# All eight down matrices of the second expert loop loaded once, and picked by a register on TensorE

## The reference, cut to what matters

```python
router_logits = x @ gate_weight.T                      # 1024 tokens, 8 experts
probs = softmax(router_logits)
top_v, top_i = top_k(probs, 2)                          # weights normalised to sum 1
def expert_step(acc, (gu, dp, w)):
    gate, up = split(x @ gu.T, 2)                       # gu: 1024 x 256 of one expert
    hidden = silu(gate) * up                            # 512 wide
    return acc + w[:, None] * (hidden @ dp.T)           # dp: 256 x 512 of one expert
```

## Time and profile before

| what | value |
|---|---|
| median of 3 runs | 451.12 us (450.35 to 452.25) |
| time of the profiled execution | 449.55 us |
| its span, first to last instruction | 447.8 us |
| PE busy | 401.5 us (90%) |
| DVE busy | 328.8 us (73%) |
| POOL busy | 253.9 us (57%) |
| ACT busy | 236.9 us (53%) |
| HBM read, written | 71.76 MB, 5.24 MB |
| down matrices: issues, size, median to landing | 23, 512 KB, 5.3 us |
| gate and up matrices: the same | 22, 1024 KB, 7.8 us |

### The profile page before, as it was taken

How to read it: one execution, slowest core, us unless ns; L and a number is a source line. 1 busy time by engine, 2 the same in 40 slices (tenths; PEclk the granted TensorE clock), 3 DMA queues, 4 the chain that set the end, 5 groups by cost and what they waited for, 6 DMA issues and landing times.

```text
span 447.8 us, 6054 instructions
## 1 busy us (share of the span) xinstructions
PE 401.5 (90%) x1749; PEld 263.9 (59%) x1749; DVE 328.8 (73%) x620; ACT 236.9 (53%) x478; POOL 253.9 (57%) x352
## 2 busy tenths in 40 slices
PE   7798999999899999958885899999999999976895
PEld 6576788555555555626772456666665666653554
DVE  5998779999999999889877268548546411048994
ACT  5624683566676767569973222332333222349883
POOL 5474028577888997236614466976985463124641
PEclk9999999999999999998985899999999999999998
DMA  6900006365546565000024898999999985150011
GB/s 215 415 32 0 1 1 220 114 218 189 164 172 229 190 202 195 0 2 2 1 94 151 272 350 284 325 364 357 322 337 359 322 301 193 42 181 1 23 37 36
DMA packets 23664, 77.39 MB, mean 173 GB/s; under 512 B 3440, under 2 KB 7920, under 8 KB 20176
## 3 DMA queue, kind: packets, MB, share of 16 engines
q1 hardware_dynamic: 20336, 69.94, 44.1%
q0 software_dynamic: 2208, 6.03, 4.1%
q10 hardware_dynamic: 1088, 1.05, 0.7%
HBM read 71.76 MB, written 5.24 MB: 172 GB/s over the span
## 4 chain that ended last, share of the span: by engine, by line
PE 50%; DVE 27%; issue 12%; POOL 4%; ACT 3%; DMA 3%; SPq 0%; DVEq 0%; POOLq 0%; ACTq 0%
PE bank L1990 9%; PE bank L2021 9%; PE bank L2001 9%; DVE hx L1295 5%; PE bank L1770 5%; DVE fw L1084 4%; DVE bw L1087 3%; PE bank L1615 2%; PE bank L1617 2%; PE bank L1616 2%; PE bank L2012 2%; DVE fw L1092 2%; PE bank L1692 2%; DVE gl L1574 2%; PE bank L1839 1%
## 5 line engine op out<-in xcount | busy, mean ns | idle before, releaser
L1770 PE MATMUL bank<-hx,w2raw 128*128 128x512 f32 x128 | 67.2, 607 | 4.2 <-DVE hx L1295 3.3
L1510 DVE TENSOR_TENSOR hm<-bank,sl 128x512 f32<-128x512 f32 x23 | 15.8, 689 | 66.1 <-PE bank L2001 36.3
L808 ACT ACTIVATE rl<-bank 128x512 f32<-128x512 f32 x64 | 38.1, 595 | 37.9 <-PE bank L1617 37.1
L1615 PE MATMUL bank<-xlhi,w1hi 128*128 128x512 f32 x64 | 49.3, 771 | 0.0
L1990 PE MATMUL bank<-gu,xbT 128*128 128x512 f32 x92 | 45.4, 617 | 2.1 <-issue 1.6
L1295 DVE TENSOR_TENSOR hx<-bank,cwb 128x512 f32<-128x512 f32 x64 | 42.0, 658 | 3.1 <-ACT bank L812 2.9
L2021 PE MATMUL bank<-dn,hT 128*128 128x256 f32 x184 | 43.5, 379 | 0.4 <-ACT hT L931 0.4
L2021 PEld LDWEIGHTS bank<-dn,hT 128*128 128x128 f32 x184 | 34.9, 190 | 14.7 <-issue 11.1
L2001 PE MATMUL bank<-gu,xbT 128*128 128x512 f32 x92 | 43.3, 593 | 0.0
L589 POOL DMA_INDIRECT y_rows<-yb,dest_i x23 | 24.5, 1066 | 32.9 <-ACT yb L937 28.8
L937 ACT ACTIVATE yb<-bank 128x256 f32<-128x256 f32 x23 | 8.8, 384 | 60.8 <-PE bank L2021 60.8
(11 more groups left out here) (307 smaller groups left out, 961.3 us busy)
## 6 DMA issues: line engine op xcount, KB each, us to landing
gu<-in_gu SPq DMA_DIRECT2D x22, 1024.0 KB, 7.8
cwb<-cw_rows SPq DMA_DIRECT2D x32, 512.0 KB, 4.0
dn<-in_dn SPq DMA_DIRECT2D x23, 512.0 KB, 5.3
traw<-in_t SPq DMA_DIRECT2D x3, 1024.0 KB, 7.1
w1raw<-in_w SPq DMA_DIRECT2D x8, 256.0 KB, 4.7
w2raw<-in_w SPq DMA_DIRECT2D x8, 256.0 KB, 4.4
kT<-in_kt SPq DMA_DIRECT2D x4, 256.0 KB, 5.1
x<-in_x SPq DMA_DIRECT2D x2, 512.0 KB, 6.8
```

Of the source, the lines that this page charges most:

```text
L808: act.activation(rl[:, u % 3, :], bank[u % 4][:], ACT.Relu).then_inc(sem("r_ready"), 1)
L1615: pe.matmul(out, lhs[0], rhs[0], start=start, stop=False)
L1770: pe.matmul(bank[4 + s][:], w2raw[:, e // 4 % 2, e % 4, :], hx[:, 0, u % 4, :], start=(e == 0), stop=(e == E0 - 1), skip_group_check=True) ...
```

## The change

The tile `dn` now holds all eight down matrices (4 MB, 32 KB in each partition) and lies at the start of the region. `gu` comes behind it, and the tiles of layer 1 and 3 that lay behind both now begin at `gu`. SP loads the eight matrices with four DMAs of 1 MB right after the router's weights, when layer 0 is done (`x1_ready` 4). `down_weights` and its 23 loads, 23 register reads and 23 waits leave SP's list. TensorE reads the owner of block b - 1 into a register of its own in each pass with b of 1 or more, behind the transposes and ahead of `up(b)`, and `block_down` addresses the matrix with it. TensorE waits for the loads of `dn` once, at block 0.

```diff
@@ -172,8 +172,9 @@
 
 
         cursor[0] = region
+        dn = sb("dn", [P, E2, I2 // P, C])
+        first_region = cursor[0]
         gu = sb("gu", [P, RING, KC, 2 * I2])
-        dn = sb("dn", [P, RING, I2 // P, C])
         region2 = cursor[0]
 
 
@@ -195,7 +196,7 @@
         ends.append(cursor[0])
 
 
-        cursor[0] = region2
+        cursor[0] = first_region
         qf = sb("qf", [P, 2, C])
         qT = sb("qT", [P, 2, KC, P], BF16)
         xp = sb("xp", [P, 2, HID])
@@ -362,6 +363,9 @@
             ternary_in(0)
             sp.wait_ge(sem("x1_ready"), 4)
             sp.dma_start(rtraw[:], rt_d).then_inc(sem("rt_in"), 16)
+            for e in range(0, E2, 2):
+                sp.dma_start(dn[:, e:e + 2, :, :], dn_d[e:e + 2, :, :, :].rearrange("e p k n -> p e k n")
+                             ).then_inc(sem("dn_in"), 16)
             for b in range(B):
                 sp.wait_ge(sem("cond_ready"), 8 + b + 1)
                 sp.dma_start(cond_d.rearrange("(t p) c -> p t c", p=P)[:, 2 * b:2 * b + 2, :],
@@ -380,27 +384,17 @@
                 n = slice(up * I2, up * I2 + I2)
                 sp.dma_start(gu[:, b % RING, :, n], gu_d[bass.ds(e, 1), :, :, n].rearrange("o p k n -> p (o k) n")
                              ).then_inc(sem(f"gu_in{b % RING}" if up else "half_in"), 16)
-
-            def down_weights(b):
-
-                e = sp.value_load(owner_i[b:b + 1, 0:1], min_val=0, max_val=E2 - 1)
-                wait(sp, sem("d_done"), b - RING + 1)
-                sp.dma_start(dn[:, b % RING, :, :], dn_d[bass.ds(e, 1), :, :, :].rearrange("o p k n -> p (o k) n")
-                             ).then_inc(sem(f"dn_in{b % RING}"), 16)
 
             sp.wait_ge(sem("owner_step"), 3)
             up_weights(0)
             half_weights(HALVED, 0)
             sp.wait_ge(sem("xb_in0"), 16)
             half_weights(HALVED, 1)
-            down_weights(0)
             sp.wait_ge(sem("xb_in1"), 16)
-            down_weights(1)
             for b in range(2, NB):
                 if b == 2:
                     sp.wait_ge(sem("xb_in2"), 16)
                 up_weights(b)
-                down_weights(b)
                 if b in (8, 14):
                     ternary_in((1, 8, 14).index(b))
             sp.wait_ge(sem("y_out0"), 16 * ((NB + 1) // 2))
@@ -2012,13 +2006,26 @@
                         ins = pe.transpose(hidden_bank(half)[:, j * P:j * P + P], hm[:, b % 2, c * P:c * P + P], ident[:])
                     ins.then_inc(sem("ht_ready"), 1)
 
+            owners = {}
+
+            def load_owner(b):
+
+                if b == 0:
+                    pe.wait_ge(sem("owner_step"), 3)
+                owners[b] = pe.value_load(owner_i[b:b + 1, 0:1], min_val=0, max_val=E2 - 1)
+
+            def own_down(b, j):
+
+                return dn[:, bass.ds(owners[b], 1), j, :].rearrange("p o n -> p (o n)")
+
             def block_down(b):
-                pe.wait_ge(sem(f"dn_in{b % RING}"), 16 * (b // RING + 1))
+                if b == 0:
+                    pe.wait_ge(sem("dn_in"), 16 * (E2 // 2))
                 wait(pe, sem("y_ready"), b)
                 for j in range(4):
                     if j % 2 == 0:
                         pe.wait_ge(sem("hT2_ready"), 2 * b + j // 2 + 1)
-                    ins = pe.matmul(y_bank(b), hT2[:, b % 2, j, :], dn[:, b % RING, j, :], start=(j == 0), stop=(j == 3))
+                    ins = pe.matmul(y_bank(b), hT2[:, b % 2, j, :], own_down(b, j), start=(j == 0), stop=(j == 3))
                 ins.then_inc(sem("d_done"), 1)
 
             keep_going(bank[3][:], 9, every[:], q1w[:, 0, 0:512])
@@ -2030,6 +2037,8 @@
                     turn_block_hidden(b - 1)
                 if b + 1 < NB:
                     turn_block(b + 1)
+                if b >= 1:
+                    load_owner(b - 1)
                 if b < NB:
                     up(b)
                 if b >= 1:
```

## The result

The changed kernel takes 445.96 us (median of 6 runs, 445.09 to 447.76). The kernel before took 450.69 us beside it (6 runs, 449.71 to 452.25).

What follows compares the result with a forecast made beforehand. TensorE was taken to set the pace, transfers close behind. Gaps of -1.62 plus 0.10 for the last address step gave -1.5 us, moving the median from 451.12 to 449.6; range 447.9 to 454.5.

Steps and rivals of the forecast that it cites:

- The register read: On TensorE's sequencer in each pass, behind the hm wait: 0.74 us, hidden by the lead, taken as zero.
- The address steps: Four register addresses in block_down, 37 ns each, about 0.6 us with their surroundings: hidden, taken as zero.
- The uncovered step at the loop's end: Down of block 22, behind its wait on hT2: the first address step adds 0.1 us (0.04 to 0.2).
- (c): Rival: PE's register read does not overlap with its queue, 0.8 us in each of 23 passes, 468 us; chance 0.12.
- (d): Rival: matmuls with a register address dispatch slowly, so down stretches, 462 us, mild form 454; chance 0.08.
- (b): Rival: the second gap, at gate(15), stays, since SP stands at traw; 450.5 us, chance 0.12.
- In all other passes the weights are in time: Expert loop: only two gates wait for gu, so hardly anything beyond 1.62 us can be won.
- 1.57 us under the median of the runs: Where the profiled execution lay; the same distance took the forecast from 448.0 to a median of 449.6 us.
- rival (e): More than the two gaps: 12 MB less read, gathers of xb or the tail profit too; 448.0 or less, chance 0.08.
- the two gaps at 1.62 us: Idle time of 0.72 us at gate(2) and 0.90 us at gate(15), waiting for gu: both removed.
- the gap at gate(15): 0.90 us removed: gu(15) issued at 326.3, 0.5 us earlier, and landing by 333 to 334 with less traffic ahead.
- the load in layer 1: Four DMAs of 1 MB at about 185 to 200 us: cost zero, bounds -0 and +0.3.

Runs made afterwards that it cites:

- e8: The changed kernel without registers on TensorE: block b takes the down matrix of expert b modulo 8; 445.33 us, ratio 0.9901.
- e12: The changed kernel with no edit, a third profile; the profiled execution took 446.06 us.
- e5: The changed kernel, with SP keeping the old down_weights register reads and waits but no load of dn; 447.0 us, ratio 0.993.
- e9: The old kernel with no edit, one more profile; the profiled execution took 453.15 us.
- e2: The changed kernel with no edit, a second profile; 446.69 us, ratio 0.9898, its profiled execution 446.21 us.
- e4: The changed kernel, with SP also keeping the old reads, waits and loads of down matrices, into buffers no product reads; 452.46 us, ratio 1.0016.
- e3: The old kernel with only SP's list reordered, gu(b) ahead of dn(b - 1), all dn loads kept; 448.09 us, ratio 0.9927.
- e7: The old kernel with SP's list reordered as in e3, and 14 in place of 9 idle products ahead of the first block; 447.3 us, ratio 0.9929.
- e11: The old kernel with no edit, one more profile; the profiled execution took 450.89 us.

## Why the prediction was wrong

**Right.** PE sets the pace, and behind the first gate the loop gains by late weights alone. Gate(2) and gate(15) follow without a gap. The register read was forecast at some 0.74 us, behind the `hm` wait and hidden: 307 + 151 ns and what lies between them, the same pass length, and e8 as a second proof. The address steps, 37 ns by SP's rows, are 46 ns. The uncovered step at the loop's end, 0.10 us, measured 0.10. The slower rivals (c) and (d) are refuted by the pass of 5.81 us, (b) by gate(15).

**Wrong: "In all other passes the weights are in time. The change can win these two gaps, 1.62 us, and hardly anything else in the loop."** This step took one execution for all of them, and so priced the wait of late weights too low. Over five profiles the late gates come to 2.1 to 6.2 us, 3.8 on average, mostly at gate(9), for which the first profile shows 0.5 us of slack, and the prediction didn't ask what would happen if the queue took 1 us longer. The text itself held the sign that this execution was mild: it lay 1.57 us under the median of the runs. The prediction carried that distance over as a constant, when it was the very thing that the change removes. The time measured is what rival (e) named, 448.0 or less, with a chance of 0.08 and the reason "so little is left"; it looked for the gain in the gathers and the tail, not in other late gates.

**Mis-sized: the two gaps at 1.62 us.** They measured 2.08. A gap cost more than its idle time: the pass lost 0.16 us beyond it at both gates, and the next pass 0.07.

**Closed for another reason than forecast: the gap at gate(15).** The forecast took the queue ahead of gu(15) as gone: issue at 326.3, landing by 333 to 334, so 7 to 8 us. It took 9.9, against 10.7 before. The landing at 333.7 looks like a hit, but by then the loop runs 2.40 us ahead of the old one (gate(13) at 322.51 instead of 324.91). Counted from gate(13), the issue came 0.57 us earlier, as forecast, and the landing 1.4 us earlier. That closed a gap of 0.90 with little to spare: gu(15) landed 0.6 us ahead of its gate (at 334.31 in the chain). At gu(2) a wait was overlooked: SP stood 1.0 us at the gather of block 2 before it could issue, and gu(2) went out at 250.61, not near 249.4. It landed 6.0 us later and in time.

**Mis-sized: the load in layer 1, at zero.** In the chain, from the last update of x in layer 0 to the start of the routing's wait of 14.6 us (184.30 to 225.39 in the first profile), it is 41.08 to 41.09 us in the four old profiles with a granted clock of 0.96 there (184 to 225 us). With the load it is 41.83 us in e12, 41.35 in e5 and 41.61 in e8 at that same clock, so 0.3 to 0.7 us longer; at 0.92 it is 41.48 without it (e9) and 41.45 and 42.44 with it (the first profile after, e2), and at full clock 41.09 with it (e4). The bound was +0.3. What holds layer 1 up was not taken apart.

**Missing: the clock of the first gate, 1.69 us.** In the five profiles of the old kernel PE was idle 1.47 to 1.58 us ahead of the first block and the gate ran at 1.2 GHz; in the three of the changed kernel it was idle 0.47 to 1.12 us and ran at 2.4. The experiments fit the same line but for e4: 1.20 us and 1.2 GHz in e3, 0.70 to 0.85 us and 2.4 GHz in e5, e7 and e8. In e4 the idle time was 0.79 us, but there the clock had not risen at all: its granted clock is 0.50 from 244 to 254 us, where that of the first old profile was 1.00 at 246 to 248 us and 0.50 again at 249 to 251 us. The rows to see the half rate were there; that it could change was not to be read from them.

Why this idle time is shorter is only partly shown. The gather of the first rows took 4.21 to 4.45 us in the old kernel and 3.91 to 4.10 in the changed one, and the nine idle products ahead of it, the same in both, took 3.23 to 3.49 us and 3.47 to 4.00, where the clock rose later (0.52 and 0.56 at 246 to 248 us in e2 and e12, with 4.00 and 3.95 us). The loads of `dn` in the loop are not the cause, for the first goes out only when the first gate has begun (249.36 against 248.24). Nothing in SP's list ahead of it differs but the load in layer 1, and e4 has that too. Yet all seven profiles with loads of `dn` in the loop and nine idle products had the low clock, and all six without such loads the full one. So the cause stays open, and with it how much of these 1.69 us belongs to the change.

## What to carry to other kernels

A transfer that lands within half a us of its use in one profile can be late in others: gu(9) was, in four out of four. The changed kernel has one of these itself, gu(15), 0.6 us ahead of its gate. List the slack of every load of a loop, not only the waits, and look at a second profile, or at least at where the profiled execution stands among the runs: one below the median understates what contention costs. When a load waits on SP behind another one's buffer, reordering the issues may bring most of what removing the bytes brings; here 3.5 of 4.9 us. And the register read of TensorE's sequencer cost nothing here, where it falls behind a wait that is released well ahead of the engine: by 3.1 us, from 324.2 to 327.28 in the rows of before.

## What the runs showed of the hardware

TENSOR_LOAD from SBUF took TensorE's sequencer 307 ns (first one 484), SyncE's 272 ns (the longest 476). The Trainium skill ("Runtime: NRT & Kernel Launch", section Instruction fetch mechanics) gives about 200 ns per register for loads from HBM; no run here loads one from there, and from SBUF it is somewhat more. A product with its address in a register took as long as one without (379 ns in both), and the address step was 46 ns in the sequencer.

The same load of 1 MB, in the same place behind the same others, took 9.4 to 12.6 us to land in five executions of one kernel, with the DMA engines at 0.92 to 0.95 over 284 to 302 us. In the changed kernel they were at 0.77 over the same stretch, and the load took 7.1 to 7.9 us in three.

TensorE's granted clock fell from 1.00 to 0.57 behind 2.15 us without a matmul in e9, between busy stretches, and stayed up behind 1.85 us in e11 and 2.19 us in e4.
